# Whole numbers joined in bf16 in the first cross-attention, and three more units made ahead of the second

## The reference

```python
def _qdq(x):
    s = jnp.maximum(jnp.max(jnp.abs(x), axis=-1, keepdims=True) / 127.0, 1e-08)
    return jnp.clip(jnp.round(x / s), -127.0, 127.0) * s
q = _qdq(x) @ _qdq(wq).T + bq
kv = cond @ wkv.T + bkv
attn = jax.nn.softmax(jnp.einsum('bnhd,bmhd->bhnm', q, k) * scale, axis=-1)
o = jnp.einsum('bhnm,bmhd->bnhd', attn, v).reshape(B, N, C)
out = _qdq(o) @ _qdq(wp).T + bp
```

## Time and profile before

| what | value |
|---|---|
| time of the runs shown | median 731.47 us of 3 (729.82 to 732.44) |
| the profiled execution | 730.61 us |
| its span, first to last instruction | 728.8 us |
| PE busy | 683.2 us, 94% of the span |
| DVE, ACT, POOL busy | 419.5, 279.1, 76.5 us |
| X0's batch loop | from 44.99 us |
| X1's batch loop | from 446.97 us |

### The profile page before, as it was taken

One profiled execution on the slowest core, in us unless ns is written; L12 is line 12 of the kernel. 1 busy time (PEld: TensorE's weight loads), 2 busy tenths in 40 slices (PEclk: granted clock), 3 DMA queues, 4 the chain that ended last, 5 costly groups with the idle time before them and its releaser, 6 DMA issues.

```text
span 728.8 us, 21897 instructions
## 1 busy us (share of the span) xinstructions
PE 683.2 (94%) x9706; PEld 450.7 (62%) x9706; DVE 419.5 (58%) x976; ACT 279.1 (38%) x508; POOL 76.5 (10%) x139
## 2 busy tenths in 40 slices
PE   5999999999997899999988979999999998899876
PEld 3656566656665667777766546676676775356654
DVE  5224447566565555555553692554977775355567
ACT  1334434434343233333422844444344454111125
POOL 1020000001000111111111332000201002000000
PEclk9999999999999999999999999999999999999999
DMA  6232101012300810000001510111291000000000
GB/s 191 87 149 36 58 31 31 31 60 85 121 2 2 289 31 31 30 31 30 2 1 59 204 58 30 61 32 59 79 301 58 2 4 1 3 4 4 3 1 30
DMA packets 39358, 42.26 MB, mean 58 GB/s; under 512 B 12704, under 2 KB 29856, under 8 KB 39008
## 3 DMA queue, kind: packets, MB, share of 16 engines
q1 hardware_dynamic: 39264, 40.86, 17.9%
HBM read 40.33 MB, written 0.52 MB: 56 GB/s over the span
## 4 chain that ended last, share of the span: by engine, by line
PE 80%; DVE 13%; ACT 3%; issue 2%; DMA 1%; POOL 1%; SPq 0%; DVEq 0%; POOLq 0%; ACTq 0%
PE psum L363 14%; PE psum L369 13%; PE psum L1048 7%; PE psum L430 5%; PE psum L383 4%; PE psum L408 4%; PE psum L397 4%; PE psum L1095 4%; PE psum L1054 4%; PE psum L1747 2%; PE psum L1079 2%; PE psum L1766 2%; DVE arena L1372 1%; PE psum L1068 1%; PE psum L1726 1%
## 5 line engine op out<-in xcount | busy, mean ns | idle before, releaser
L363 PE MATMUL psum<-arena 128*128 128x512 f32 x256 | 125.8, 618 | 10.4 <-DMA ident<-in_ident 8.1
L369 PE MATMUL psum<-arena 128*128 128x256 f32 x512 | 123.4, 386 | 0.0
L369 PEld LDWEIGHTS psum<-arena 128*128 128x128 f32 x512 | 93.2, 190 | 20.8 <-issue 8.2
L363 PEld LDWEIGHTS psum<-arena 128*128 128x128 f32 x256 | 45.6, 194 | 55.0 <-issue 41.8
L628 ACT ACTIVATE arena<-arena 128x512 f32<-128x512 f32 x64 | 48.6, 806 | 71.1 <-DVE arena L750 71.1
L430 PEld LDWEIGHTS psum<-arena 128*17 128x17 f32 x4096 | 39.3, 96 | 35.5 <-issue 30.3
L622 ACT ACTIVATE arena<-psum,arena 128x512 f32<-128x512 f32 x64 | 42.5, 687 | 37.9 <-DVE arena L737 37.8
L737 DVE TENSOR_REDUCE arena<-psum 128x1 f32<-128x512 f32 x64 | 42.4, 684 | 22.7 <-PE psum L383 22.6
L750 DVE TENSOR_SCALAR arena<-psum 128x512 f32<-128x512 f32 x64 | 41.2, 685 | 22.4 <-PE psum L397 20.2
L1048 PE MATMUL psum<-y_cols,arena 128*128 128x512 f32 x112 | 52.2, 599 | 0.0
L430 PE MATMUL psum<-arena 128*17 128x32 f32 x4096 | 48.6, 195 | 1.8 <-DVE arena L773 0.5
(11 more groups left out here) (232 smaller groups left out, 997.9 us busy)
## 6 DMA issues: line engine op xcount, KB each, us to landing
arena<-in_ctxT SPq DMA_DIRECT2D x32, 512.0 KB, 3.7
arena<-in_L_attn_Wv SPq DMA_DIRECT2D x1, 2048.0 KB, 8.3
arena<-in_L_attn_Wq SPq DMA_DIRECT2D x8, 256.0 KB, 2.9
arena<-in_L_attn_Wk SPq DMA_DIRECT2D x8, 256.0 KB, 3.4
arena<-in_L_attn_Wo SPq DMA_DIRECT2D x1, 2048.0 KB, 11.5
arena<-in_L_ffn_w_gating SPq DMA_DIRECT2D x1, 2048.0 KB, 7.6
arena<-in_L_attn_wo SPq DMA_DIRECT2D x1, 2048.0 KB, 11.0
arena<-in_wq_upT SPq DMA_DIRECT2D x1, 1536.0 KB, 8.6
```

What stands on the lines that cost most here:

```text
L363: last = nc.tensor.matmul(bank, wkv[:, c, i * P:(i + 1) * P], x[:, c, :], start=(c == 0), stop=(c == NC - 1))
L369: last = nc.tensor.matmul(bank[:, kk * D:(kk + 1) * D], x[:, c, k * P:(k + 1) * P], wkv[:, c, D:2 * D], start=(c == 0), stop=(c == NC - 1))
```

## The change

It has four parts.

1. **Whole numbers in bf16 (X0).** `qdq_rows` becomes `whole_rows`, which ends at the rounded whole number and writes it as bf16. The weights, the tokens and the attention's output stay whole numbers through their turning (an ordinary matmul with a bf16 identity), the queries and the output product. The scales come in afterwards: by token and channel for the queries (`token_scales`, two DVE products, then ACT adds the bias), and by row and channel for the output (`channel_scales`, a product in `residual`).
2. **X0's order.** In the loop `turn_out` stands behind two `turn`s, and `out_rows` behind two `values`.
3. **The start.** The transfers of the key weight and the first context come first; PE no longer waits for the identity there; `first_busy` gives it three f32 matmuls on constants, and ACT one small instruction, before data is there.
4. **X1's units.** 24 ahead instead of 21: 4 and 5 at the end of A0, 6 to 19 in F0, 20 to 23 ahead of the loop. Then three a batch in batches 0 to 9 and two in 10 to 14. A seventh home for keys and values lies in the first 2112 words of the arena, so M1's weights are loaded one batch of values later (`4 * 7`).

```diff
-    ((12040, 26500), (26500, 39000), (39000, 41112)),
+    ((12040, 26500), (26500, 39000), (39000, 41112), (0, 2112)),
-def qdq_rows(nc, ch, rows, n, q):
+def whole_rows(nc, ch, rows, n, q, whole):
     ch.link(nc.vector.tensor_scalar(rows, rows, ROUND, 127.0, ALU.subtract, ALU.min))
-    for i in range(n):
-        ch.mark(nc.vector.tensor_scalar(rows[:, i, :], rows[:, i, :], -127.0, q.s[:, i:i + 1], ALU.max, ALU.mult))
-    ch.join()
+    ch.link(nc.vector.tensor_scalar(whole, rows, -127.0, None, ALU.max))
...
-        for dst, src in ((wkv[:, :, 0:D], cols(d.wkT)), (wkv[:, :, D:2 * D], cols(d.wvT))):
-            sp.dma_start(dst, src).then_inc(s_kv_in, 16)
+        sp.dma_start(wkv[:, :, 0:D], cols(d.wkT)).then_inc(s_wk, 16)
         load_ctx(sp, 0)
+        sp.dma_start(wkv[:, :, D:2 * D], cols(d.wvT)).then_inc(s_kv_in, 16)
...
-        u = FIRST + 3 * b + k + (max(b - 1, 0) // 4 if L0 else 0)
-        return None if (k == 3 and (not L0 or b % 4 or not b)) or u >= 4 * NB else u
+        if not L0:
+            u = FIRST + 3 * min(b, FULL) + 2 * max(b - FULL, 0) + k
+            return None if k >= (3 if b < FULL else 2) or u >= 4 * NB else u
...
         scores_rows(pe, b, 0)
-        turn_out(pe, tile_at(b, OUT))
         if b:
             turn(pe, b - 1, 2), turn(pe, b - 1, 3)
+        turn_out(pe, tile_at(b, OUT))
         unit_pe(pe, slot(b, 0))
-        out_rows(pe, tile_at(b, TAKE))
         if b:
             values(pe, b - 1, 2), values(pe, b - 1, 3)
+        out_rows(pe, tile_at(b, TAKE))
...
+    def turn_tokens(pe, k):
+        ts = f.groups[k]
+        pe.wait_ge(e.s_y, f.y + ts[-1] + 1)
+        for c in range(NC):
+            for j, t in enumerate(ts):
+                a = (c * len(ts) + j) * P
+                last = nc.tensor.matmul(O[k][:, a:a + P], whole[:, t, c * P:(c + 1) * P], identb, start=True, stop=True)
+        last.then_inc(e.s_yT, 1)
+    def token_scales(pe):
+        pe.wait_ge(s_wT_out, 1)
+        for t in range(NT):
+            nc.tensor.matmul(TOKENS[:, t * P:(t + 1) * P], qx.s[:, t:t + 1].to_broadcast([P, P]), e.ident, start=True, stop=True)
+    def channel_scales(pe):
+        pe.wait_ge(s_wT_out, 2)
+        pe.wait_ge(s_qT_out, 2)
+        for c in range(NC):
+            last = nc.tensor.matmul(CHANNELS[:, c * P:(c + 1) * P], qp.s[:, c:c + 1].to_broadcast([P, P]), e.ident,
+                                    start=True, stop=True)
+        last.then_inc(s_wT, 1)
...
+            e.ch.link(nc.vector.scalar_tensor_tensor(out=orow[:, t, :], in0=OUTB[:, D:2 * D], scalar=qx.s[:, 0:1], in1=swp,
+                                                     op0=ALU.mult, op1=ALU.mult))
             v.wait_ge(s_xb, t + 1)
-            nc.vector.tensor_tensor(e.X[:, t, :], OUTB[:, D:2 * D], e.X[:, t, :], ALU.add).then_inc(s_res, 1)
+            nc.vector.tensor_tensor(e.X[:, t, :], orow[:, t, :], e.X[:, t, :], ALU.add).then_inc(s_res, 1)
...
+            v.wait_ge(s_qT, 1)
+            e.ch.link(nc.vector.tensor_copy(pr[0], TOKENS))
+            for c in range(NC):
+                v.wait_ge(s_qT, c + 1)
+                nc.vector.scalar_tensor_tensor(out=qT[:, c, :], in0=B[4 + c], scalar=swq[:, c:c + 1], in1=pr[0],
+                                               op0=ALU.mult, op1=ALU.mult).then_inc(s_small, 1)
...
         out_rows(pe, H - 1)
+        for u in units(4, 5):
+            e.phases[X1].unit_pe(pe, u)
...
-        out_rows(pe, HT - 2)
-        out_rows(pe, HT - 1)
-        for u in units(14, 15, 16):
+        for h in range(HT - 2, HT):
+            for u in units(17 - HT + h):
+                e.phases[X1].unit_pe(pe, u)
+            out_rows(pe, h)
+        for u in units(17, 18, 19):
             e.phases[X1].unit_pe(pe, u)
...
+def first_busy(nc, e, bank, n):
+    for _ in range(n):
+        nc.tensor.matmul(bank, e.neghalf[:, 0:1].to_broadcast([P, P]), e.neghalf[:, 0:1].to_broadcast([P, 512]),
+                         start=True, stop=True)
...
-                        sp.wait_ge(phases[X1].s_pv, 4 * 6)
+                        sp.wait_ge(phases[X1].s_pv, 4 * 7)
...
-            pe.wait_ge(s_const, 16)
+            pe.wait_ge(s_half, 1)
+            first_busy(nc, e, e.B[5], 3)
```

More of the change, by code:

```diff
@@ L238, in xattn @@
     qT = take([P, NC, ROWS])
-    orow, orT = take([P, NT, D]), take([P, NC, P])
+    orow, orT = take([P, NT, D]), take([P, NC, P], BF16 if L0 else F32)
     rc = take([P, 4, H])
@@ L242, in xattn @@
     if L0:
-        q = Named(m=take([P, NT]), s=take([P, NT]), r=take([P, NT]))
+        qx, qq, qp = (Named(m=take([P, NT]), s=take([P, NT]), r=take([P, NT])) for _ in range(3))
+        wq8 = take([P, NC, D], BF16)
+        wp8 = wq.rearrange("p c n -> p (c n)").bitcast(BF16)[:, 0:NC * D].rearrange("p (c n) -> p c n", c=NC)
+        whole, yT8 = take([P, NT, D], BF16), take([P, NC, ROWS], BF16)
+        identb, swq, swp = take([P, P], BF16), take([P, NC]), take([P, D])
         nmx = take([P, HG])
@@ L405, in turn @@
         pe.wait_ge(s_exp, 4 * b + g + 1)
+        if b == 0 and g == 0:
+            pe.wait_ge(s_wT_out, 3)
         wait(pe, (s_pT_act, s_pT_dve)[g % 2], 2 * b + g // 2)
@@ L456, in turn_out @@
         for c in range(NC):
-            last = nc.tensor.transpose(OUTB[:, c * P:(c + 1) * P], orow[:, t, c * P:(c + 1) * P], e.ident)
+            cols = slice(c * P, (c + 1) * P)
+            if L0:
+                last = nc.tensor.matmul(OUTB[:, cols], whole[:, t, cols], identb, start=True, stop=True)
+            else:
+                last = nc.tensor.transpose(OUTB[:, cols], orow[:, t, cols], e.ident)
         last.then_inc(s_orT, 1)
@@ L530, in queries @@
             for c in range(NC):
-                last = nc.tensor.matmul(B[4 + c2], wqT[:, c, c2 * P:(c2 + 1) * P], e.yT[:, c, :],
+                last = nc.tensor.matmul(B[4 + c2], wqT[:, c, c2 * P:(c2 + 1) * P], (yT8 if L0 else e.yT)[:, c, :],
                                         start=(c == 0), stop=(c == NC - 1))
@@ L542, in pe @@
             for k in range(2):
-                norm_turn(nc, pe, e, f, k, O[k])
-            pe.wait_ge(s_wT_out, 1)
+                turn_tokens(pe, k)
+            token_scales(pe)
             queries(pe)
@@ L548, in pe @@
                 unit_pe(pe, u)
-            pe.wait_ge(s_wT_out, 2)
+            channel_scales(pe)
         else:
@@ L1170, in act @@
         copy_oT(act, H - 1)
-        for u in units(2, 3):
+        for u in units(2, 3, 4, 5):
             e.phases[X1].unit_act(act, u)
@@ L1328, in pe @@
     def pe(pe):
-        for u in units(4, 5):
+        for u in units(6):
             e.phases[X1].unit_pe(pe, u)
@@ L1336, in pe @@
         for h in range(HT):
-            for u in units(6 + h):
+            for u in units(7 + h):
                 e.phases[X1].unit_pe(pe, u)
@@ L1359, in act @@
             nc.scalar.activation(gl[h % 2], gb[h % 2], ACT.Gelu_apprx_tanh).then_inc(s_gelu, 1)
-            for u in units(6 + h):
+            for u in units(7 + h):
                 e.phases[X1].unit_act(act, u)
-        for u in units(14, 15, 16):
+        for u in units(15, 16, 17, 18, 19):
             e.phases[X1].unit_act(act, u)
@@ L2069, in _ @@
         def _(act):
+            act.wait_ge(s_half, 1)
+            nc.scalar.activation(warm, e.neghalf2, ACT.Identity)
             for i, phase in enumerate(phases):
```

79 lines of the change are left out of this document (51 added, 28 removed).

## The result

The changed kernel takes **718.72 us** (median of 4 runs, 717.91 to 719.58), the kernel before beside it 730.64 (728.18 to 732.44): ratio 0.984, 95% interval 0.982 to 0.986. A second comparison on another chip gave 0.985 (0.983 to 0.987). Forecast were 716.7 us, 711.5 to 722.0, and "faster" with 0.97: range and direction held, the gain is 2 us smaller than the sum said. The profiled execution took 717.91 us, its span is 716.1 against 728.8. Three of the profiles further down (after_again, no_first_busy and combo2) come from executions with a lower granted clock throughout (0.75 to 0.85): nothing is read from them but what is said, and such executions are left out of every time and ratio given here.

What follows compares the result with a forecast made beforehand. PE, busy 94% of the span, was taken as the bound, with its idle and slow places read. Terms -7.1 - 4.2 - 0.4 + 0.0 - 3.1 = -14.8 from 730.6 gave 715.8, plus 0.86 for the median 716.7 us; range 711.5 to 722.

Steps and rivals of the forecast that it cites:

- Term 1: Start: first unit no longer waits for the identity, PE at full rate as if from 6.5 instead of 11.1: -4.5 us.
- Term 2: X0's prologue: bf16 queries -2.75, turned weights -0.4, new channel_scales +0.4 us.
- Term 3: X0's tiles: 1.4 us saved in each of batches 6, 10 and 14, -4.2; last tile -0.4.
- Term 4: A0 and F0: three units made ahead fit into PE's idle time, 0.0 us, between -0.5 and +1.5.
- Term 5: X1's loop with three units fewer, limited by the chain through DVE and POOL: -3.1 us.
- Batch 12 starts 1.0 earlier: X1: a unit and its copy leave the chain to batch 12, while PE stands about 3 us there.
- Batch 8, -0.25: X1: in the chain to batch 8, batch 6 loses a copy (-1.0) and batch 7 gains one (+0.75).
- Batches 12 and 13 lose a unit, batch 14 gains one, -1.8: X1's last batches: fewer units shorten the loop by 1.8 us, with DVE less than a batch behind.
- the rival that I gave 0.20: X1: the granted clock falls in the new wait ahead of batch 12, costing 1.7 us, giving 718.4; chance 0.20.
- a loop in X1 that gains nothing: DVE holds X1's batches 12 to 14 too, or F0's units cost time: 718.2 to 719.5 us; chance 0.12.
- the signs that I had named for a wrong prediction: X1's wait missing, granted clock dropping behind it, X0's unit 14 waiting long for ACT, or F0's end over 1 us later.
- My own case: Whole kernel as the summed terms say, stated as 714.7 to 718.7 us; chance 0.49.

Runs made afterwards that it cites:

- after_again: The changed kernel again with no edit, as measure for the other kernels on its chip: 718.05 us, ratio 0.985.
- no_first_busy: The changed kernel without the three starting matmuls on constants, transfer order kept: 719.83 us, ratio 0.986.
- combo2: The changed kernel with POOL's separated queries earlier, M1's weights asked for later and DVE's weight slices placed elsewhere in X1: 713.93 us, ratio 0.978.
- units_old: The changed kernel with X1's units placed as before (21 ahead, then three a batch in batches 0 to 13): 719.12 us, ratio 0.986.
- x0_old_order: The changed kernel with X0's finished-tile steps where they stood before, all still in bf16: 719.78 us, ratio 0.986.
- pool_both: The changed kernel with POOL making X1's next separated queries earlier in batches 4, 7 and 11: 719.52 us, ratio 0.986.
- fill12: The changed kernel with twelve identity multiplications on PE ahead of X1's batch 12 wait: 717.38 us, ratio 0.984.
- m1_later: The changed kernel with M1's weights asked for one batch of values later, behind both last contexts: 718.75 us, ratio 0.986.
- slices_moved: The changed kernel with DVE's eight last-layer weight slices moved from X1's batches 6-13 to 5, 6, 8, 9, 12-15: 719.75 us, ratio 0.987.
- slices_pool: The changed kernel with the moved slices of slices_moved and POOL's order of pool_both: 716.10 us, ratio 0.982.
- rows_first: The changed kernel with X0's out_rows back ahead of the two values: 719.41 us, ratio 0.986.
- combo2_fill: combo2 plus seven identity multiplications on PE ahead of the last tile's turning in X0: 712.97 us, ratio 0.977.

## Why the prediction was right, and where its terms were not

**Term 1** held, and was 0.6 too small. I set `first_busy` at 0.81 to 0.86 a record and its end at 6.1. Its first records do step 0.85 or more, but the pace rose within the fourth, some 3 us after the first matmul (0.73 each on average), and it ended at 5.28. That moment is luck: in units_old, with the same start, all six are at half pace and the first unit starts at 6.17, as forecast. In the ten profiles with this start X0's first scores come at 36.90 to 37.94. The pace in no_first_busy shows that these matmuls, not the earlier data, bring full pace.

**Term 2** held in each part: the queries -2.7, the two turned weights -0.4, `channel_scales` +0.5. The turned weight steps 0.22 for four bf16 records of 128 columns, 55 ns each (19.71 to 19.93 in the trace). By the Trainium skill (TensorE: Matmul & The Clock Gate, Back-to-back issue gap) it would be 81; this trace disagrees for bursts of four (and of eight, L551: 0.45 us), and the measurement decides.

**Term 3**'s mechanism held, its size was 1.3 too large. "0.7 + 0.1 = 0.8" for bf16 was right (0.86, 0.63, 0.85 by x0_old_order). The step that failed is the first: "the wait of 0.59 goes, since two turns now stand where it was; that is also what hides DVE's rounding", three times. The wait was 0.59 in all three batches and is gone ahead of the turned tile in all three, but I took PE's side alone. On DVE the rounding still stands ahead of the copy that the values need, with A0's preparation between them in batches 10 and 14 and an odd unit too in batch 10, and PE meets that delay one step later: 0.84 us in batch 10, 0.25 in batch 14, none in batch 6. The order was worth 0.7 in all, not 1.8.

**Term 4** came out at -1.3 instead of 0.0, and that is the clock. Before, it falls behind the last tile of X0 (0.54 in the earlier trace rows); in the changed kernel's profile it doesn't. From X0's last tile to F0's first, the profiles of the changed unit order take 157.8 us without the fall (changed kernel, pool_both, fill12, x0_old_order) and 159.0 to 159.4 with it (m1_later, slices_moved, slices_pool, rows_first). Less these 1.4, the term is about 0.0, as forecast; that the fall did not come in the changed kernel's profile is luck.

**Term 5** failed: -3.1 forecast, 0.0 measured. By its own steps:
- "Batch 12 starts 1.0 earlier": batches 10 and 11 together are 1.1 shorter. Right, and so was the wait of about 3 us (3.04).
- "Batch 8, -0.25": batch 7 is 0.5 shorter.
- Missed: batch 4 is 0.68 longer. POOL's all-reduce waits for DVE's batch 3, which by the swapped parity has two units where it had one (it starts 2.4 us into batch 4, before 0.1), and the next batch's separated queries stand behind the all-reduce and nearly 7 us more of POOL. In pool_both batch 4 is 9.76 again. I had not read POOL's order at batch 4.
- Missed: 0.47 in batch 9, the stall without a releaser.
- "Batches 12 and 13 lose a unit, batch 14 gains one, -1.8": measured +0.4. Of the 2.2 between them 1.6 are the clock behind the 3 us wait (10.36 against 8.73 in fill12), which is the rival that I gave 0.20, at its price of 1.7; most of the rest is a wait of 0.45 for ACT in batch 12.

So the sum came within 2.1 us with larger errors in it: 3.1 in term 5 and 1.3 in term 3 one way, 0.6, 1.3 and 0.3 (term 1, term 4, and M1 with F1) the other. The 1.3 of term 4 is a clock fall that happened not to come. Two of the rivals came true together, the fall in the new wait and a loop in X1 that gains nothing; that the first one's 718.4 lies so near the time measured is luck of the same kind. The granted clock behind that wait is also one of the signs that I had named for a wrong prediction: the time was in the range, this step was not. (My own case, "from 714.7 to 718.7 by the bounds of terms 1 and 4", is a slip: these bounds give 715.1 to 720.7.)

What lies under both rivals is one thing, the chain through DVE. With DVE's slices placed around the tile's work the loop is 3.7 us shorter (slices_moved), and with POOL's order too 4.5 to 5.3 us (combo2_fill, slices_pool); 1.7 of each is the fall that no longer comes. The old unit order was not tried with them. It is argued, not shown, that it would not do as well: PE is busy for 139.6 us in that loop before, so that at least 2.8 us of the gain need the units made ahead.

## What to carry to other kernels

When PE is given less work in a stretch whose end another engine sets, nothing is gained, and the wait that appears can cost a clock fall on top: find which engine's queue is behind at that place, and move its deferrable work, before taking work from PE. A step moved out of the way of a late input meets the same lateness at the next consumer in that engine's order, so follow the late engine's queue, not the waiting one's. After removing one wait, read the next one in the same batch: here POOL, then ACT behind DVE, then the last batch stood one behind another.

## What the runs showed of the hardware

**Falls of the clock are single events with one price.** In ten of the eleven profiles that could be read throughout, before the last microseconds of the span, there are one to three of them (none in combo2_fill's), and each takes 1.70 or 1.71 us from PE's pace (two stand together in slices_moved and x0_old_order); the kernel loses that or less, 1.4 at the end of X0, where other waits stand behind it. They begin within waits of PE of 1.0 to 3.5 us or less than 2 us behind them, single waits or two close together, and not each time: behind the wait for the last tile of X0 (1.2 us in the kernel before, 1.7 in the others), the clock fell in six profiles of ten and stayed up in four; and of the two kernels with waits of 1.5 and 1.4 us at the end of F0 it fell there in units_old and not in the kernel before. The Trainium skill (TensorE: Matmul & The Clock Gate, What's actually happening) says that the monitor runs free of the program; by that rule the trace agrees, since the same wait goes either way. The falls are also part of the scatter: combo2's runs took 710.7, 712.5, 713.9, 716.4 and 717.4 us at mean granted clocks of 0.999, 0.996, 0.994, 0.992 and 0.993, of which the clock makes up at most 5 of the 6.7 us. The five of combo2_fill don't follow it (711.4 at 0.999, but 714.3 at 0.998 and 713.0 at 0.994), so that something else scatters too. Differences of 2 us between single profiles of this kernel mean nothing until the falls are counted.

**A stall of PE without a releaser** came in the same place of batch 9, behind the 28th of 32 values, in six profiles with M1's weights loading at that time (0.24 to 1.96 us; in a seventh, slices_pool, the row is 0.3 us longer), where a 16 KB packet of the instruction queue lands among them; with the weights asked for later it was gone there, and two of 0.8 us stood where they load now. In all eight of these stalls PE goes on 2.6 to 2.9 us after the start of such a packet, and the later the packet starts in batch 9, the longer is the stall: 0.24 us in the changed kernel, where it starts 2.6 us behind the batch's first scores, 1.96 in pool_both, where it starts 4.3 behind. In the kernel before and in units_old, where M1's weights load there too, it starts 2.2 and 2.3 us behind them, and PE does not stall. The Trainium skill (Runtime: NRT & Kernel Launch, Instruction fetch mechanics) says that such a fetch is mostly hidden; in these places it was not. Full DMA engines are not needed for it: in M1, in ten of the eleven profiles, the kernel before among them, PE stands once or twice for 0.3 to 1.0 us without a releaser (0.80 in the changed kernel at 668.76, among matmuls on small tiles), goes on 2.2 to 2.9 us after the start of such a packet, and no other transfer runs in the 4 us ahead. That the packet is what PE waited for rests on these times; no run moved a packet alone.
